# Another order for the opening of a fused cross-attention and expert kernel

## The reference

```
a   = layernorm(x)
q   = qdq(a) @ qdq(wq).T + bq                  # qdq: int8 fake quantisation per row
k,v = split(ctx @ wkv.T + bkv)                 # ctx: 1601 context rows per batch
o   = softmax(q k^T / sqrt(32)) v              # 16 heads of 32
x   = x + tanh(g0) * (qdq(o) @ qdq(wp).T + bp)
x   = x + tanh(g1) * (moe(layernorm(x)) + shared(layernorm(x)))
```

## Time and profile before

| | us |
|---|---|
| median of 3 runs (3244.9 to 3255.8) | 3248.48 |
| the profiled execution | 3254.07 |
| its span | 3251.4 |
| end of the last k_lo of the first keys | 76.2 |
| first reduce of the first maxima | 97.52 |
| first scores | 135.82 |
| end of the first group (its heads copied) | 193.10 |
| end of the second | 255.53 |

### The profile page before, as it was taken

How to read it: one execution, slowest core, us unless ns; L and a number is a source line. 1 busy time by engine, 2 the same in 40 slices (tenths; PEclk the granted TensorE clock), 3 DMA queues, 4 the chain that set the end, 5 groups by cost and what they waited for, 6 DMA issues and landing times. The chain is left out here.

```text
span 3251.4 us, 42577 instructions
## 1 busy us (share of the span) xinstructions
PE 2811.8 (86%) x14876; PEld 1192.9 (37%) x14876; DVE 1727.0 (53%) x2854; ACT 1387.3 (43%) x2460; POOL 1806.8 (56%) x1570
## 2 busy tenths in 40 slices
PE   5898988899889888988899898889888689996986
PEld 3223333333333333333333333333332344443765
DVE  6566556656565656566556655665653324342222
ACT  3155445644564455455545544564456211010111
POOL 0285566556655665657566656755669223324555
PEclk9799999899999999999999999999999789998999
DMA  4111012110211031103112101211011221222997
GB/s 127 33 44 52 21 34 70 52 35 20 78 48 44 11 97 39 34 21 92 29 34 69 52 21 34 69 52 34 21 51 29 79 89 66 78 78 73 271 279 194
DMA packets 146578, 215.53 MB, mean 66 GB/s; under 512 B 24984, under 2 KB 78232, under 8 KB 146368
## 3 DMA queue, kind: packets, MB, share of 16 engines
q1 hardware_dynamic: 130496, 195.95, 20.0%
q0 software_dynamic: 15872, 16.87, 2.8%
HBM read 126.49 MB, written 34.24 MB: 49 GB/s over the span
## 5 line engine op out<-in xcount | busy, mean ns | idle before, releaser
L1510 POOL TENSOR_TENSOR prob_acc<-prob_acc,probs 128x512 f32<-128x512 f32 x1152 | 1430.1, 1275 | 484.7 <-ACT probs L1038 484.2
L1038 ACT ACTIVATE probs<-s_ps 128x512 f32<-128x512 f32 (+1 forms) x1664 | 939.0, 596 | 806.8 <-PE s_ps L810 787.3
L1253 DVE TENSOR_REDUCE piece_max<-r_all 128x2 f32<-128x802 f32 (+1 forms) x1024 | 965.2, 986 | 229.1 <-PE r_all L732 223.6
L810 PE MATMUL s_ps<-q_stack,k_flat 97*128 97x512 f16 (+1 forms) x1664 | 630.0, 397 | 73.9 <-ACT probs L1038 66.0
L732 PE MATMUL r_all<-k_flat,q_stack 96*128 96x401 f16 (+1 forms) x2048 | 552.3, 353 | 131.7 <-DVE piece_max L1253 80.2
L824 PE MATMUL o_ps<-probs,v_sb 128*32 128x512 f32 (+1 forms) x3328 | 462.8, 629 | 21.4 <-ACT probs L1038 21.4
L810 PEld LDWEIGHTS s_ps<-q_stack,k_flat 97*128 97x128 f16 (+1 forms) x1664 | 161.5, 102 | 635.6 <-ACT probs L1038 411.5
L1507 POOL COPY prob_acc<-probs 128x512 f32<-128x512 f32 x128 | 72.8, 612 | 507.2 <-PE sum_ps L844 372.2
L732 PEld LDWEIGHTS r_all<-k_flat,q_stack 96*128 96x128 f16 x2048 | 178.3, 100 | 392.7 <-DVE piece_max L1253 143.1
L1542 POOL DMA_INDIRECT slot_rows<-payload,slot x128 | 125.3, 979 | 317.7 <-DVE slot L1440 194.7
L1246 DVE SCALAR_TENSOR_TENSOR k_lo<-r_all,bk_col,k_hi 128x400 f16<-128x400 f32 (+1 forms) x128 | 81.8, 639 | 280.7 <-ACT k_hi L996 280.7
(11 more groups left out here) (193 smaller groups left out, 2752.8 us busy)
## 6 DMA issues: line engine op xcount, KB each, us to landing
k_flat<-k_hi SPq DMA_DIRECT2D x256, 100.1 KB, 2.2
ctx_raw<-in_ctx SPq DMA_DIRECT2D x96, 256.0 KB, 2.9
v_sb<-in_L_ffn_w SPq DMA_DIRECT2D x48, 512.0 KB
xin<-in_x SPq DMA_DIRECT2D x16, 1024.0 KB, 5.6
k_flat<-k_lo SPq DMA_DIRECT2D x128, 100.1 KB, 2.2
ctx_hi<-in_L_ffn_w SPq DMA_DIRECT2D x24, 512.0 KB
ctx_lo<-in_L_ffn_w SPq DMA_DIRECT2D x24, 512.0 KB
q_stack<-q_hi SPq DMA_DIRECT2D x256, 32.0 KB, 1.8
```

Source lines behind the costliest of these rows:

```text
L810: nc.tensor.matmul(s_ps[j % SBANKS][0:w, :], k_stack[:, g % 2, j, kt * P:kt * P + w], q_stack[:, g % 2, j, :], start=True, stop=True).then ...
L1038: nc.scalar.activation(probs[0:w, slot, j, :], s_ps[j % SBANKS][0:w, :], ACT.Exp).then_inc(probs_ready, 1)
L1253: V.reduce_max(piece_max[:, j * TT + qt, 2 * i:2 * i + 2], r_all[:, k:k + 2, 0:MAX_WIDE[i]], X_AXIS).then_inc(free_of(*key), 1)
L1510: last = G.tensor_tensor(prob_acc[:, j, :], prob_acc[:, j, :], probs[:, slot, j, :], ALU.add)
```

## The change

The opening gets another order, on every engine.

- SP loads wk, wv, three contexts, wq and x first, then the small vectors, then the rest. wk, wv and wq have a third of `probs` each, and wp goes to `work`, issued after the last context.
- The ring begins with wkT and wvT, then contexts. wqT (four tiles) comes after context 4, and its quantisation on VectorE after context 3. A key piece comes as soon as the last context that it reads has been transposed (after contexts 3, 6, 9 and 12).
- No `v` tile stands among the contexts. Two come ahead of the maxima, seven among them (after every fourth), and the last four within the first group at steps 5, 7, 8 and 10. The first nine are copied by ScalarE and get their bias from POOL.
- wp is scaled at step 2 and rounded at step 3 of the first group; its transposes come at step 6, gate weights and scales at step 7.
- The ones of `k_stack` are set by POOL. The tanh of the two gates stands behind context 0 on ScalarE; it waits for all eight small loads.

```diff
+FIRST_V, WQ_AFTER = 9, 3
+WP_SCALE, WP_ROUND, WP_TURN = 2, 3, 6
...
+    if g == 0:
+        tiles += [("v", b, t) for t in V_AT if V_AT[t] == kt and (b or t >= FIRST_V)]
+    if (b, g) == (0, 0):
+        tiles += [("setup", "wpT", c) for c in range(DC)] if kt == WP_TURN else []
+        tiles += [("setup", "gateT"), ("setup", "swp")] if kt == WP_TURN + 1 else []
...
+def last_context(i):
+
+    return (PIECE_AT[i] + PIECE[i] - 1) // P
 
 
 def first_tiles():
 
-    order = []
+    order = [("setup", name, c) for name in ("wkT", "wvT") for c in range(DC)]
     for t in range(KT):
         order.append(("ctxT", 0, t))
-        if values_after(t) is not None:
-            order.append(("v", 0, values_after(t)))
-    left = [("v", 0, t) for t in range(KT) if ("v", 0, t) not in order]
-    return order + key_tiles(0, 0) + x_tiles(0) + [("q", 0, 0)] + left + max_tiles(0, 0) + [("maxT", 0, 0)]
+        if t == WQ_AFTER + 1:
+            order += [("setup", "wqT", c) for c in range(DC)]
+        order += [("k", 0, 0, i) for i in range(PIECES) if last_context(i) == t]
+    order += x_tiles(0) + [("q", 0, 0)] + [("v", 0, t) for t in range(2)]
+    maxima = max_tiles(0, 0)
+    for n, key in enumerate(maxima):
+        order.append(key)
+        order += [("v", 0, t) for t in range(2, FIRST_V) if (t - 1) * len(maxima) // (FIRST_V - 1) == n]
+    return order + [("maxT", 0, 0)]
...
+            for name in ("wk", "wv"):
+                sp.dma_start(raw[name], w_v[name]).then_inc(raw_w_in[name], DMA)
+            for t in range(CT_SLOTS):
+                context_in(0, t)
+            sp.dma_start(raw["wq"], w_v["wq"]).then_inc(raw_w_in["wq"], DMA)
+            sp.dma_start(xin[:, :, :], x_v[0]).then_inc(x_in, DMA)
...
+            for t in range(CT_SLOTS, KT):
                 context_in(0, t)
+            sp.dma_start(raw["wp"], w_v["wp"]).then_inc(raw_w_in["wp"], DMA)
             stacks(0, 0)
...
+            def gates():
+
+                act.wait_ge(small_in, 8 * DMA)
+                nc.scalar.activation(tanhs[:, :], tanhs[:, :], ACT.Tanh).then_inc(tanh_ready, 1)
...
+                elif kind == "v" and b == 0 and key[2] < FIRST_V:
+                    t = key[2]
+                    w = rows(t)
+                    ps = full(act, *key)
+                    nc.scalar.copy(v_sb[0:w, t, :], ps[0:w, :]).then_inc(first_v_copied, 1)
+                    act.wait_ge(first_v_copied, t + 1)
+                    act.sem_inc(free_of(*key), 1)
...
             for key in first_tiles():
                 tile(key)
+                if key == ("ctxT", 0, 0):
+                    gates()
...
+            def query_weights():
+
+                dve.wait_ge(raw_w_in["wq"], DMA)
+                quantise(probs[:, 2], swq).then_inc(wq_int_ready, 1)
...
+            def output_weights(at):
+
+                if at == WP_SCALE:
+                    dve.wait_ge(raw_w_in["wp"], DMA)
+                    row_scales(work, swp)
+                elif at == WP_ROUND:
+                    for c in range(DC):
+                        full(dve, "xT", 0, c)
+                    quantise_rows(work, range(TT)).then_inc(wp_int_ready, 1)
...
+                if key == ("ctxT", 0, WQ_AFTER):
+                    query_weights()
+                if key == ("ctxT", 0, KT - 1):
+                    small_constants()
...
+            step.mark(G.memset(k_stack[KSPLIT:KSPLIT + 1, :, :, :], 1.0))
+            step.settle()
+            pool.sem_inc(ones_ready, 1)
+            pool.wait_ge(small_in, 8 * DMA)
+            for t in range(FIRST_V):
+                pool.wait_ge(first_v_copied, t + 1)
+                G.tensor_tensor(v_sb[:, t, :], v_sb[:, t, :], bv_row[:, :], ALU.add).then_inc(first_v_ready, 1)
```

More of the change, by code:

```diff
@@ L174, in __init__ @@
     def __init__(self):
-        order = [("setup", name, c) for name in ("wqT", "wpT", "wkT", "wvT") for c in range(DC)]
-        order += [("setup", "gateT"), ("setup", "swp")]
-        order += first_tiles()
+        order = first_tiles()
         for at in steps():
@@ L476, in _ @@
                    "wv": wkv[D:2 * D, :].rearrange("(r p) d -> p r d", p=P)}
[L477 to L497, removed]
+            raw = {"wk": probs[:, 0], "wv": probs[:, 1], "wq": probs[:, 2], "wp": work[:, :, :]}
             def context_in(b, t):
@@ L647, in _ @@
                     close(last, "setup", name, c)
-            for w, name in enumerate(("wkT", "wvT")):
-                pe.wait_ge(raw_w_in[w], 2 * DMA)
-                for c in range(DC):
+                elif name in ("wkT", "wvT"):
+                    w = 0 if name == "wkT" else 1
+                    pe.wait_ge(raw_w_in[name[0:2]], DMA)
                     ps = open_tile("setup", name, c)
@@ L654, in _ @@
                     close(last, "setup", name, c)
[L655 to L664 removed]
+                elif name == "gateT":
+                    pe.wait_ge(small_in, 8 * DMA)
+                    ps = open_tile("setup", "gateT")
+                    for r in range(DC):
+                        last = nc.tensor.transpose(ps[:, r * E:(r + 1) * E], gate_raw[:, r * P:(r + 1) * P], ident[0:E, 0:E])
+                    close(last, "setup", "gateT")
+                elif name == "swp":
+                    ps = open_tile("setup", "swp")
+                    for r in range(4):
+                        last = nc.tensor.matmul(ps[:, r * P:(r + 1) * P], swp[:, r:r + 1].to_broadcast([P, P]), ident[:, :],
+                                                start=True, stop=True)
+                    close(last, "setup", "swp")
             def int_transposes(name, b, c, dst=None):
@@ L1134, in _, with setup_tile @@
             step.mark(V.memset(gsum[:, :, :], -3.0e38))
-            step.mark(V.memset(k_stack[KSPLIT:KSPLIT + 1, :, :, :], 1.0))
-            for w, scale in enumerate((swq, swp)):
-                dve.wait_ge(raw_w_in[w], DMA)
-                if w:
-                    for c in range(DC):
-                        full(dve, "setup", "wqT", c)
-                quantise(probs[:, w], scale).then_inc(w_int_ready, 1)
-            for w, name in enumerate(("wkT", "wvT")):
-                for c in range(DC):
+            def setup_tile(name, c=None):
+                if name in ("wkT", "wvT"):
+                    w = 0 if name == "wkT" else 1
                     ps = full(dve, "setup", name, c)
@@ L1220, in tile @@
                                     ctx_hi[:, :, t * P:t * P + w], ALU.subtract).then_inc(free_of(*key), 1)
-                elif kind == "v":
+                elif kind == "v" and (b or key[2] >= FIRST_V):
                     t = key[2]
```

100 lines of the change are left out of this document (58 added, 42 removed).

## The result

The changed kernel takes **3276.98 us** (median of 5 runs, 3274.17 to 3283.75), the kernel before 3244.9 beside it (3239.12 to 3255.8): ratio **1.0097 [1.0073, 1.0121]**, slower by about 1%. I had forecast 3254 with a range to 3269. In later comparisons the kernel before had medians of 3249.62, 3247.93 and 3247.95 over 11, 23 and 18 runs, so the loss is 27 to 32 us. The profiled execution took 3280.81 us with a span of 3279.0, against 3254.07 and 3251.4.

A forecast was written before the change was run, and what follows sets the result against it. VectorE was taken to bound the start and first maxima, TensorE the V stretch and groups. First-group start -9.6, added work +12.8, bank wait +3.0 gave +6.2 us: 3260 profiled, 3254 as median; range 3239 to 3269.

The forecast's parts named there:

- The maxima with seven V tiles among them: First maxima: each V tile adds 2.37 us, one runs 1.9 longer; 47.3 us instead of 30.9.
- What the first group takes on: First group: 12.8 us of added TensorE work at full length, plus 3 for a bank wait at wp's quantisation.
- The rest moves only: Everything behind the first group only shifts in time; the second group stays at 62.4 us.
- The new start: Opening up to the last key piece: last k_lo ends at 60.5 instead of 76.2, 15.7 us earlier (bounds 50 and 66).
- To the first maximum: From last key piece to first reduce: 12.05 us instead of 21.3, so the first reduce comes at 72.5.
- rival A: Among the maxima, the clock falls between V tiles, each 1.8 us longer: +18, 3266 us; chance 0.22.
- The tail: Queries and first key piece after the maxima: V keeps the clock up, saving 1.0 us (0 to 2).
- Rival B: The first group swallows the added work, leaving -9.6 alone: 3239 us; chance 0.14.
- C: Short opening: small loads land before 15, key pieces overlap, last piece at 50: 3244 us; chance 0.16.
- nothing waits: POOL's memset of the ones (13 us, ending near 18) and its nine V additions hold nothing up.

The follow-up runs named there:

- a4: Changed kernel with the last four V tiles ahead of the maxima and none in the first group; 3269.61 us, 1.0066 of the kernel before.
- b2: Changed kernel with wp scaled and rounded right behind the first queries, before the first maxima; 3267.44 us, 1.0062 of the kernel before.
- a3: Changed kernel with the tanh behind the last context on ScalarE instead of behind the first; 3269.61 us, 1.0072 of the kernel before.
- c2: Changed kernel with a V tile after every third maximum instead of every fourth; 3265.47 us, 1.0058 of the kernel before.
- b4: Kernel before with only one part of the change, the ones set by POOL instead of VectorE; 3245.36 us, 0.9997 of the kernel before.
- c3: Kernel before with the ones set by POOL, only after both quantisations; 3241.53 us, 0.9974 of the kernel before.
- b1: Changed kernel, V 0-5 among contexts, 6-12 and wp's transposes ahead of maxima, wp quantised behind first queries, tanh last; 3242.9 us, 0.9982 of before.
- c1: b1 with V 0-4 one to a context, 5-10 ahead of maxima, 11 and 12 at step 2, tanh behind context 3; 3240.31 us, 0.9976 of before.
- c4: c1 with contexts and V tiles in turn, four key pieces in one block behind them, wq quantised behind context 0; 3237.82 us, 0.9964 of before.
- a1: Changed kernel with wp scaled at step 0 and rounded at step 1 of the first group; 3277.89 us, 1.0085 of the kernel before.

## Why the prediction was wrong

Two steps failed in their size: **"The maxima with seven V tiles among them"** (47.3 us for a measured 53.5) and **"What the first group takes on"** (15.8 us, 12.8 and 3.0, for a measured 22.6). A third failed outright: **"The rest moves only."** The forecast of +6.2 us at the start of the second group came out as +20.8, and behind it another 7 to 8 us were lost, in the profile's span as in the median. What was lost up to the end of the first group would alone have left the time at 3269, the edge of the range. The 14.6 between them (the group's rows count from its first score; there it grew by 22.6, from 57.3 to 79.8):

| step | predicted | measured | off by |
|---|---|---|---|
| first reduce | 72.5 | 75.17 | +2.7 |
| maxima | 47.3 | 53.5 | +6.2 |
| tail, row_max to first score, against before | -1.0 | -2.0 | -1.0 |
| group, four V tiles | 10.4 | 10.9 (a4) | +0.5 |
| group, quantisation of wp | 3 | 6.8 (b2) | +3.8 |
| group, transposes, gate, scales | 2.4 | 4.8 (the rest of 22.6) | +2.4 |

1. *The new start.* The terms were mostly right. The tanh wait ended at 19.81 instead of 18, and behind it context 3 was late, since SP's issues of the small vectors stood still, which I hadn't priced at all: I had read only the rate. Key pieces took 3.6 to 4.0 us, as said; the last one fell to half pace halfway, against my full clock. 63.74 for 60.5, within my bounds and, by the spread of this opening (60.67 to 64.17), no clear miss. a3 doesn't show that the tanh's place cost any of it.
2. *To the first maximum.* 11.43 us from key piece to reduce for 12.05.
3. *The maxima.* The mechanism was right and its price exact: 2.38 a tile for 2.37. The size was off in the clock. I let one tile run slow, 1.9 us; four did, 2.1 + 3 x 1.7 = 7.2 over the 2.38. Reduces were 29.7 for 28.8. This is half of rival A, which had all tiles slow from the second on; in fact every second one is. c2 shows that the clock, not the tiles, was this part: at one V to three maxima the extra 7.2 falls to 2.4. Why the clock falls behind four maxima and not behind three stays open. That the four banks make the price of 2.38 is worked out from the waits; no kernel with another ring was run.
4. *The tail.* Right in kind: q and keys at full clock (1.00 in the window 128:133, 0.51 before).
5. *The first group.* V cost its full length. The quantisation block was mis-sized: I counted how late the third maximum would be (3 us; it was 4.49), and nothing for TensorE's clock behind such an idle time. In this window of the changed kernel the granted clock is 0.66, with VectorE busy for 7.87 of 10 us:

```profile
160.00:170.00 10.00, 7.63 (x27) 2.34 (x28) 7.87 (x11) 2.79 (x5) 2.81 (x3) 0.66 0.00 0
```

Part of it was also POOL: 2.58 us for the four instructions of 155.90 to 158.48, which take 1.67 with POOL idle. That wp's transposes make maxima wait for their banks (0.47 and 0.67 us, idle behind `wpT`) is in the trace; that this and the clock make up the whole 2.4 is argued, not shown; and the 2.4 is not far above the 1.3 us by which this group differs from profile to profile.

Rival B (the group swallows the additions) is refuted by a4; C (last piece at 50) by the last key piece, which no opening of this study had before 60. That "nothing waits" for POOL's memset of the ones was true of the changed kernel, where VectorE reads PSUM beside it, and false of b4: the sentence held by the place, not by the reason I gave. It took 10.77 us, not 13.

**What stays open.** "The rest moves only" rested on later groups whose code doesn't change. The median lost 27 to 32 us, the first group's end 20.8. In the profiles the 31 later groups take 2343.7 us after and 2335.5 before; over all kernels of this study they lie between 2323.6 and 2343.7. Single groups differ by the granted clock; two groups of the kernel before:

```profile
648.00:725.40 77.40, 71.14 (x414) 27.61 (x412) 40.39 (x52) 35.10 (x64) 46.60 (x40) 1.00 0.09 22
955.70:1035.40 79.70, 74.13 (x414) 29.49 (x413) 40.40 (x52) 35.39 (x65) 46.63 (x40) 0.96 0.09 22
```

Same work, 2.3 us longer where the clock was granted less. Median less the first group's end is 3055 for before and b4 and 3056 for c3, but 3058 (b1, c1, c2) to 3063 (the changed kernel) for the eleven kernels with the changed code, c4 with 3061 among them. So c4 won 16.6 us in its first group and 10 in the median. The first group's end is one profile's and good to some 3 us, but the two families don't overlap.

One rival for this was not tested: the 508 added waits on TensorE. By themselves they cost nothing that these profiles show: if one takes for each of the 31 groups its shortest time, the sum is 2318.4 over the three kernels without them and 2316.2 over the eleven with them. Whether they make the clock fall more often I can't tell: the groups' sum is 2330.8 on average without them and 2335.0 with them, where single profiles of either kind lie 10 to 20 us apart. A changed kernel with the old wait in the later batches would decide it, and none was run. I can show that a longer group has the lower clock, not why.

## What to carry to other kernels

Filling a stretch that another engine bounds pays only if the filler doesn't share what hands the work over: here four PSUM banks and in-order queues made every V tile cost its length, less 0.2 us. Price what is moved by its place, not by its duration: the clock after an idle time or a gapped stretch, the engine that shares a port, and the queue in front of it each stretched instructions whose rows in the trace were short. And time the parts one by one: the ones on POOL, put behind the quantisation (c3), gained 6 us while the whole change lost about 30.

## What the runs showed of the hardware

- VectorE's `tensor_scalar` and POOL exclude each other for whole instructions: 5.95 us for 0.17 beside a memset (b4), 1.4 for 0.36 to 0.42 beside additions (a1). Reduces, and operations that read PSUM, were not held up: a reduce of 2.29 us took that beside the memset and after it (b4), four `wkv_lo` took 2.48 us beside it (the changed kernel) and with POOL idle (b4). The Trainium skill ("SBUF — State Buffer", Who interferes with whom) states that `tensor_scalar` is among the VectorE operations that can take the port pair shared with GpSimd, that whoever issues first has the pair for the whole instruction, and that on this chip a reduce never contends. The rows agree in all three.
- With V tiles after every four maxima the clock fell for every second tile, though the stretches between tiles have the same gaps; after every three it did not fall until the V tiles were over (c2). 4.49 us of idleness was followed by half pace until 168.3, for 6 us.
- SP's issue of one small vector took 4.37 us behind seven large loads, 2.31 before the change, where two large loads stood ahead of it.
- Two V tiles at step 2 of the first group cost 1.4 us (c1 and c4, against before) instead of 5.2.
- With the tanh behind context 0 or 3, ScalarE loaded a table (1.28 us) ahead of the first exponentials; with the tanh behind the last context (a3, b1) it did not.
- The same opening, run by six kernels, ended up to 3.5 us apart in single profiles; the last key piece took 2.0 us in some (a4, c2) and 3.3 in others (the changed kernel).
- A memset of one partition, 12,808 elements, takes the same on both engines: 10.73 and 10.77 us.
